# Thirty-two written-out heads, fewer and larger row transfers, two sums buffers, a longer lead and narrower exponentials in a transformer block

## The reference

```
ada = silu(c) @ Wada + bada            # shift, scale, gate for both halves
h   = ln(x) * (1 + scale_msa) + shift_msa
q, k, v = h @ Wq + bq, h @ Wk + bk, h @ Wv + bv      # reshaped to 16 heads of 32
A   = softmax(q @ k.T / sqrt(32))                    # 2048 x 2048 for each of 32 heads
x   = x + gate_msa * ((A @ v) @ Wo + bo)
h2  = ln(x) * (1 + scale_mlp) + shift_mlp
out = x + gate_mlp * (gelu(h2 @ W1 + b1) @ W2 + b2)
```

## Time and profile before

| | us |
|---|---|
| median of 3 runs | 2916.54 |
| lowest and highest of the runs | 2909.09, 2918.22 |
| the profiled execution's own time | 2912.46 |
| its span, first to last instruction | 2910.6 |
| PE busy | 2542.5 |
| POOL busy | 1505.6 |
| DVE busy | 1755.7 |
| ACT busy | 1357.1 |
| mean granted TensorE clock | 0.917 of 2.4 GHz |

### The profile page before, as it was taken

One profiled execution on the slowest core, in us unless ns is written; L12 is line 12 of the kernel. 1 busy time (PEld: TensorE's weight loads), 2 busy tenths in 40 slices (PEclk: granted clock), 3 DMA queues, 4 the chain that ended last, 5 costly groups with the idle time before them and its releaser, 6 DMA issues.

```text
span 2910.6 us, 57655 instructions
## 1 busy us (share of the span) xinstructions
PE 2542.5 (87%) x19544; PEld 1372.6 (47%) x19544; DVE 1755.7 (60%) x2878; ACT 1357.1 (47%) x1598; POOL 1505.6 (52%) x706
## 2 busy tenths in 40 slices
PE   7998868888888888888888888888888887999998
PEld 5787623333333333333333333333333333788887
DVE  5444666666566666666666666666666632665663
ACT  3322145555555555555555555555555544222211
POOL 0000146656667765666676576677566653433220
PEclk9999978989889998899998898999898988999999
DMA  7656442223222222322222232222232111311310
GB/s 260 206 177 172 118 109 50 47 64 70 51 48 47 47 47 67 69 49 47 47 47 48 66 71 47 47 47 47 64 69 50 43 39 49 88 58 58 104 40 29
DMA packets 214223, 211.01 MB, mean 72 GB/s; under 512 B 121600, under 2 KB 154368, under 8 KB 204544
## 3 DMA queue, kind: packets, MB, share of 16 engines
q1 hardware_dynamic: 213232, 207.44, 27.5%
q10 hardware_dynamic: 720, 0.02, 0.0%
HBM read 146.30 MB, written 60.82 MB: 71 GB/s over the span
## 4 chain that ended last, share of the span: by engine, by line
PE 61%; SPq 21%; DMA 6%; issue 5%; DVE 4%; ACT 3%; POOL 0%; ACTq 0%; DVEq 0%; POOLq 0%
PE ps L1245 16%; PE ps L1374 13%; SPq L489 9%; PE ps L1353 7%; SPq L496 6%; PE ps L1490 6%; PE ps L1364 5%; PE ps L1339 4%; PE ps L1355 3%; PE ps L1360 3%; PE ps L1357 2%; SPq L466 2%; SPq L470 2%; DMA partial_sums<-work 2%; DVE part_max L1069 2%
## 5 line engine op out<-in xcount | busy, mean ns | idle before, releaser
L710 POOL TENSOR_TENSOR work<-work 128x1024 f32<-128x1024 f32 x576 | 1353.3, 2386 | 775.4 <-PE ps L1364 464.1
L1069 DVE TENSOR_REDUCE part_max<-ps 128x1 f32<-128x512 f32 x1984 | 1243.4, 683 | 669.0 <-PE ps L1339 666.8
L858 ACT ACTIVATE work<-ps 128x1024 f32<-128x1024 f32 x1024 | 995.6, 1022 | 603.1 <-PE ps L1360 595.9
L1374 PE MATMUL ps<-work 128*32 128x512 f32 x4096 | 610.5, 671 | 0.0
L1339 PE MATMUL ps<-acts_r 32*128 32x512 f32 x1344 | 403.9, 504 | 101.5 <-ACT work L838 84.4
L1245 PE MATMUL ps<-acts_r,weights_r 128*128 128x512 f32 x1536 | 381.2, 398 | 4.9 <-DVE acts_r L989 3.8
L1353 PE MATMUL ps<-acts_r 32*128 32x512 f32 x1408 | 336.0, 504 | 38.6 <-DVE work L1002 18.7
L1353 PEld LDWEIGHTS ps<-acts_r 32*128 32x128 f32 x1408 | 141.6, 199 | 412.8 <-ACT work L858 339.3
L1245 PEld LDWEIGHTS ps<-acts_r,weights_r 128*128 128x128 f32 x1536 | 291.6, 191 | 69.7 <-issue 6.8
L1360 PE MATMUL ps<-acts_r,minus_r 1*128 1x512 f32 x1024 | 237.7, 462 | 65.3 <-DMA acts_r<-max_T 65.3
L1360 PE MATMUL ps<-m_odd,minus_r 1*128 1x512 f32 x1024 | 232.6, 457 | 56.8 <-DMA m_odd<-max_T 56.8
(11 more groups left out here) (88 smaller groups left out, 2478.7 us busy)
## 6 DMA issues: line engine op xcount, KB each, us to landing
acts_r<-k_hi SPq DMA_DIRECT2D x130, 256.0 KB, 4.6
acts_r<-k_lo SPq DMA_DIRECT2D x129, 256.0 KB, 4.8
work<-in_x SPq DMA_DIRECT2D x16, 1024.0 KB, 5.7
q_hi<-work SPq DMA_DIRECT2D x32, 256.0 KB, 2.6
q_lo<-work SPq DMA_DIRECT2D x32, 256.0 KB, 3.3
k_hi<-work SPq DMA_DIRECT2D x32, 256.0 KB, 2.6
k_lo<-work SPq DMA_DIRECT2D x32, 256.0 KB, 3.2
v_rows<-work SPq DMA_DIRECT2D x32, 256.0 KB, 2.0
```

Of the source, the lines that this page charges most:

```text
L710: nc.gpsimd.tensor_tensor(psum_acc[:, at], first, prob[:, t % RING, at], ALU.add).then_inc(add_ok, 1)
L858: nc.scalar.activation(prob[:, t % RING, h * (2 * CH):(h + 1) * (2 * CH)].rearrange("p (j q) -> p j q", q=CH), ps[:, S_BANK + 2 * h:S_BANK ...
L1069: nc.vector.tensor_reduce(part_max[:, r * TT + q // NQ, q % NQ:q % NQ + 1], ps[:, bank, :], AX.X, ALU.max).then_inc(a_max, 1)
L1374: mm = nc.tensor.matmul(ps[j * DH:(j + 1) * DH, O_BANK, :], v_sb[k % TWO][:, t, :], prob[:, t % RING, j * CH:(j + 1) * CH], start=(t == 0) ...
```

## The change

The change has six parts, all in the attention stage.

1. All 32 heads are written out; the loops and their registers are gone.
2. `load_k` is one transfer in place of four: its source is 32 rows read four times over, its destination all 128 partitions. `load_q` is one in place of four as well. The shift rows of a head take four transfers in place of 16.
3. `sums` has two buffers, used in turn, each with its own semaphore (in the last head one buffer alone).
4. The max pass leads by three steps in place of two, so it is complete in step 12; head 0 has three additional quads of it, in steps 2, 6 and 10.
5. ACT's exponentials are 512 wide, four in a step, and PE waits for each score bank by itself.
6. One table lists the uses of all seven banks. PE's order of matmuls within a step is as it was.

```diff
 HI_BUF, TWO = 3, 2
-PERIOD = 6
 M_ROW = 3 * DH
 POOL_TILES = [0, 1, 3, 4, 6, 7, 9, 10, 12, 13]
 PE_TILES = [t for t in range(NT) if t not in POOL_TILES]
 NADD = len(POOL_TILES) - 1
 ND = len(PE_TILES) + 1
 HALVES = 2
-PAIRS = 2
 FILLS = NQ * NT
-LEAD = 2
-EXTRA_AT = (3, 8)
-A_BANKS, S_BANK, O_BANK = 3, 3, 7
+LEAD = 3
+EXTRA_AT = (2, 6, 10)
...
-            tile = (t - 1) % NT
-            if (g or t) and tile in PE_TILES:
-                step["sums"].append((PE_TILES.index(tile), *use("D", 2 if g == G - 1 else None)))
-            if g and t == 1:
-                step["sums"].append((ND - 1, *use("D", 2 if g == G - 1 else None)))
-            steps.append(step)
+            d_bank = 2 if g == G - 1 else None
+            uses = {"extra": [], "max": [None] * NQ, "scores": [use("S", 3 + r) for r in range(NQ)], "sums": []}
+            if g == 0 and t in EXTRA_AT:
+                uses["extra"] = [use("M") for n in range(NQ)]
+            if g < G - 2 or g == G - 2 and t < NT - LEAD:
+                for r in (2, 3, 0, 1):
+                    uses["max"][r] = use("M")
+            tiles = [(t - 1) % NT] if (g or t) and (t - 1) % NT in PE_TILES else []
+            groups = [PE_TILES.index(tile) for tile in tiles] + ([ND - 1] if g and t == 1 else [])
+            uses["sums"] = [(d, *use("D", d_bank)) for d in groups]
+            steps.append(uses)
         heads.append(steps)
-    last_tiles = [(PE_TILES.index(NT - 1), *use("D", 2)), (ND - 1, *use("D", 2))]
-    return heads, last_tiles
...
-        AFTER = ROUNDS * PERIOD + 1
+
+        SUMS_END = USES[G - 1][0]["sums"][0][3]
+
+        def sums_buffer(n):
+            return (n - 1) % 2 if n < SUMS_END else 0
+
+        def sums_before(n, b):
+
+            return sum(sums_buffer(m) == b for m in range(1, n))
...
             def load_k(dst, src, g, done):
-                for r in range(NQ):
-                    sp.dma_start(dst[r * DH:(r + 1) * DH, :].bitcast(F32), src[1][bass.ds(g * DH, DH), :]).then_inc(done, 16)
+                rows = src[1][g * DH:(g + 1) * DH, :].rearrange("(o d) q -> o d q", o=1).broadcast_to((NQ, DH, L))
+                sp.dma_start(dst.bitcast(F32), rows).then_inc(done, 16)
 
             def load_q(dst, src, g, done):
-                for r in range(NQ):
-                    sp.dma_start(dst[r * DH:(r + 1) * DH, :].bitcast(F32), src[0][bass.ds(g * DH, DH), r * CH:(r + 1) * CH]).then_inc(done, 16)
+                rows = src[0][g * DH:(g + 1) * DH, :].rearrange("d (r q) -> r d q", q=CH)
+                sp.dma_start(dst.bitcast(F32), rows).then_inc(done, 16)
 
...
             def put_max(g, u):
 
                 sp.wait_ge(maxT_ok, g + 1)
+                row = m_row[u][0:P:DH, :].bitcast(F32).rearrange("r (s q) -> r s q", q=P)
                 for w in range(MAX_PIECES):
-                    for r in range(NQ):
-                        row = m_row[u][r * DH:r * DH + 1, :].bitcast(F32).rearrange("o (s q) -> o s q", q=P)
-                        sp.dma_start(row[:, :, w * DH:(w + 1) * DH],
-                                     max_T[w * DH + r * TT:w * DH + (r + 1) * TT, :]).then_inc(maxT_in, 16)
+                    sp.dma_start(row[:, :, w * DH:(w + 1) * DH], max_T[w * DH:w * DH + NT, :]).then_inc(maxT_in, 16)
 
...
-            def store_sums(i, g, uses):
+            def store_sums(g, uses):
 
                 for d, _, _, n in uses:
-                    n = i * (PERIOD * ND) + n
+                    b = sums_buffer(n)
                     sp.wait_ge(sums_ok, n)
-                    sp.dma_start(sums_dram[bass.ds(g * ND + d, 1), :].rearrange("o (r q) -> (o r) q", q=CH), sums[0:P:DH, :]).then_inc(sums_out, 16)
+                    sp.dma_start(sums_dram[g * ND + d:g * ND + d + 1, :].rearrange("o (r q) -> (o r) q", q=CH),
+                                 sums[b][0:P:DH, :]).then_inc(sums_out[b], 16)
 
             def load_sums(g):
 
-                sp.wait_ge(sums_out, 16 * ND * (g + 1))
-                sp.dma_start(sums_c[:], sums_dram[bass.ds(g * ND, ND), :].rearrange("n (p x) -> p n x", x=NT)).then_inc(sums_in, 16)
+                done = (USES[g + 1][1]["sums"] if g + 1 < G else USES_END)[-1][3]
+                for b in range(2):
+                    sp.wait_ge(sums_out[b], 16 * sums_before(done + 1, b))
+                sp.dma_start(sums_c[:], sums_dram[g * ND:(g + 1) * ND, :].rearrange("n (p x) -> p n x", x=NT)).then_inc(sums_in, 16)
 
...
+            def take_sums(g, uses):
 
                 for d, bank, _, n in uses:
+                    b = sums_buffer(n)
                     if d < ND - 1:
                         act.wait_ge(pv_mm, START + g * NT + PE_TILES[d] + 1)
                     else:
                         act.wait_ge(den_mm, START + g + 1)
-                    if n > 1:
-                        act.wait_ge(sums_out, 16 * (i * (PERIOD * ND) + n - 1))
-                    nc.scalar.activation(sums, ps[:, bank, :], ACT.Copy).then_inc(sums_ok, 1)
+                    if sums_before(n, b):
+                        act.wait_ge(sums_out[b], 16 * sums_before(n, b))
+                    nc.scalar.activation(sums[b], ps[:, bank, :], ACT.Copy).then_inc(sums_ok, 1)
 
...
 
                     last, gl = ((t - RING) % NT, g if t >= RING else g - 1)
-                    if t >= RING or k:
+                    if gl >= 0:
                         act.wait_ge(pv_mm, START + gl * NT + last + 1)
                         if last in POOL_TILES:
                             act.wait_ge(add_ok, START + gl * (NADD * HALVES) + max(POOL_TILES.index(last), 1) * HALVES)
-                    for h in range(PAIRS):
-                        act.wait_ge(b_mm, g * FILLS + t * NQ + 2 * h + 2)
-                        nc.scalar.activation(prob[:, t % RING, h * (2 * CH):(h + 1) * (2 * CH)].rearrange("p (j q) -> p j q", q=CH),
-                                             ps[:, S_BANK + 2 * h:S_BANK + 2 * h + 2, :], ACT.Exp, scale=SCALE).then_inc(exp_ok, 1)
-                    if k and t == 0:
-                        take_output(i, k - 1)
-                    take_sums(i, g if t > 1 else g - 1, A_USES[k][t]["sums"])
+                    for j, (bank, _, n) in enumerate(USES[g][t]["scores"]):
+                        act.wait_ge(b_mm, n)
+                        nc.scalar.activation(prob[:, t % RING, j * CH:(j + 1) * CH], ps[:, bank, :], ACT.Exp, scale=SCALE).then_inc(exp_ok, 1)
+                    if g and t == 0:
+                        take_output(g - 1)
...
+            def bank_free(use):
+
+                bank, before, _ = use
                 if before:
                     kind, n = before
-                    if kind == "M":
-                        pe.wait_ge(a_max, i * (PERIOD * FILLS) + n)
+                    if kind == "S":
+                        pe.wait_ge(exp_ok, START + n)
+                    elif kind == "M":
+                        pe.wait_ge(a_max, n)
                     else:
-                        pe.wait_ge(sums_ok, i * (PERIOD * ND) + n)
-
```

More of the change, by code:

```diff
@@ L62, with bank_table @@
 COL = P // 4
-LOADS_HI, LOADS_LO, LOADS_0 = 8, 9, 6
+LOADS_HI, LOADS_LO, LOADS_0 = 2, 3, 6
 MAX_PIECES = 4
-def a_sequence():
-    count = {"M": FILLS, "D": 0}
-    last = [None] * A_BANKS
+def bank_table():
+    last = [None] * BANKS
+    count = {"S": 0, "M": FILLS, "D": 0}
     turn = 0
-    heads = []
     def use(kind, bank=None):
@@ L77, in use @@
         if bank is None:
-            bank = turn % A_BANKS
+            bank = turn % 3
             turn += 1
+        before = last[bank]
         count[kind] += 1
-        before = last[bank]
         last[bank] = (kind, count[kind])
         return bank, before, count[kind]
+    heads = []
     for g in range(G):
@@ L87, in a_sequence @@
         for t in range(NT):
[L88 to L91, removed]
-            tile = (t - 1) % NT
-            if (g or t) and tile in PE_TILES:
-                step["sums"].append((PE_TILES.index(tile), *use("D", 2 if g == G - 1 else None)))
-            if g and t == 1:
-                step["sums"].append((ND - 1, *use("D", 2 if g == G - 1 else None)))
-            steps.append(step)
+            d_bank = 2 if g == G - 1 else None
[9 more added lines that the diff above has]
+            steps.append(uses)
         heads.append(steps)
-    last_tiles = [(PE_TILES.index(NT - 1), *use("D", 2)), (ND - 1, *use("D", 2))]
-    return heads, last_tiles
-A_USES, A_LAST = a_sequence()
+    end = [(d, *use("D", 2)) for d in (PE_TILES.index(NT - 1), ND - 1)]
+    return heads, end
+USES, USES_END = bank_table()
 assert NT - 1 in PE_TILES
@@ L165, in block_kernel @@
         bv_rows = view(work, 3072, D)
-        sums = view(work, 3072, CH)
+        sums = [view(work, at, CH) for at in (3072, 1024)]
         o_st = [view(work, at, CH) for at in (2048, 2560)]
@@ L271, in block_kernel @@
         sums_ok = sem("sums_ok")
-        sums_out = sem("sums_out")
+        sums_out = [sem(f"sums_out{b}") for b in range(2)]
         sums_in = sem("sums_in")
@@ L577, in _ @@
```

(26 more changed lines are left out.)

235 lines of the change are left out of this document (108 added, 127 removed).

## The result

The changed kernel takes 3029.61 us (median of 3 runs, 3022.74 to 3038.69) against 2916.54: the ratio is 1.040 (95% interval 1.034 to 1.045), so slower by 3.4 to 4.5%. The forecast was 2930 with a range of 2850 to 3190. The time lies in the range, and the waits came where they were worked out, at steps 3 and 6, but together they were longer: the increase was 113 us, not 13. The direction was little more than an even guess, as slower had a chance of 0.49.

What follows compares the result with a forecast made beforehand. Two stalls per head, 7.3 and 6.3 us, from waits for SP's transfers were to give way to one at step 6. 2912.5 + 3 (30 heads) + 11 (outside them) = 2926.5, or 2930 on the median's scale; range 2850 to 3190.

Steps and rivals of the forecast that it cites:

- Shift rows: SP's hand-over at the head boundary: four transfers take 2.5 us, 7.4 less than the 16 before.
- stall A: Head boundary of the kernel before: ACT idles while PE waits for shift rows; 7.3 us per head, forecast to go.
- Four engines: One-transfer k and q loads run on four of 16 DMA engines, 12.9 us against 5.1; chance 0.66.
- The rival of sixteen engines: Loads follow the destination and keep 5.1 us; both stalls go, 51.9 us a head, 2565 us; chance 0.14.
- The high part's load: First load in a head: 0.314 us a packet, 12.9 us with q; step 0's store lands at about 15.0.
- the packets stay slow: Rival for the k loads: 0.55 us a row, a head grows by 15 us, near 3400 us; chance 0.10.
- SP is not held: Rival: output stores are accepted at once, step 1's store lands 2.5 us earlier per head, 2855 us; chance 0.10.
- Exponentials: ACT: four of 512 take 2.10 us, 0.15 more; plain step 3.05 us, nine cost 1.4 us a head.
- The slow steps behind a stall: The step after the step 6 wait was again taken at 4.98 us, as in the kernel before.
- Written-out heads: Heads without loops and registers: taken at nothing, bounds of -1 and +1 us a head.
- The start: Before head 0: +10.5 us from the q store behind head 0's k loads, -2.8 around the v stores.
- Head 0: Its late weights queue behind two loads, 15 us more, mostly hidden; taken at +6 us (0 to 15).

Runs made afterwards that it cites:

- four_loads: The changed kernel with the k and q loads by four transfers each again, all else as changed: 2545.69 us, ratio 0.873.
- four_exp1024: four_loads with two exponentials of 1024 in a step in place of four of 512: 2526.77 us, ratio 0.867.
- four_lead2: four_loads with the max pass two steps ahead in place of three: 2539.34 us, ratio 0.871.
- four_shift16: four_loads with 16 transfers for the shift rows, lead of three kept: 2652.29 us, ratio 0.910.
- two-engine run: The changed kernel with each k and q load as two transfers, source outer dimension two: 3770.8 us, one run.

## Why the prediction was right in kind and short in size

*Shift rows and stall A: right.* The hand-over takes 2.31 us (2.5 worked out), the idle time at the boundary is 0.57, and L492 is not in the chain.

*Four engines: right.* The windows show 25% of 16. The Trainium skill, DMA: Bandwidth & Descriptors, section "Why a DMA increments its semaphore by 16 and not by 1", gives as the number of engines the largest up to 16 that divides the slowest dimension of both sides. The trace agrees: 25% with a four and 12.6% with a two against 128 and 64 partitions fit that rule, and the times of the three splits, 2545.69, 3029.61 and 3770.8 us, go the same way. The rival of sixteen engines had priced what four_loads then showed: 51.9 us a head and 2565, measured 51.0 and 2545.69.

*The high part's load: the term that was mis-sized.* The step said "On each of four engines 32 x 0.314 + 32 x 0.089 = 12.9 us" and let step 0's store land 15.0 us into the head. It landed at 1436.99 - 1416.30 = 20.7, because a packet of the high part took 0.465 us. So step 3 waited 8.5 us in place of 2.6. By that duration the load would take 32 x 0.465 + 32 x 0.089 = 17.7 us, 4.8 more than worked out, of the 5.7 by which the store was late (an estimate from one window). The low parts, behind another load, kept to 0.311. Step 1's store landed at 1452.20 - 1416.30 = 35.9 (32.2 worked out), step 6 waited 4.9 in place of seven, and this head took 66.7 us where 63.3 stood. The text had this as the rival "the packets stay slow", half of which it called as well possible: over all heads the excess is 66.0 - 63.3 = 2.7 us, 82 in all. The forecast's own part of the range ended at 0.40 us a packet; the high part alone is above it, and the mean of the two parts, 0.388, is just inside, because the low part was quick. That was not foreseen.

*The rival "SP is not held": it fell.* SP was held longer than before, 10.7 + 18.1 us a head against 6.4, with fewer transfers outstanding. It seems to be the pieces queued on the four engines, not the number of transfers, that it stands behind.

*Exponentials: nearly right.* Four take 2.06 to 2.07 us (2.10 worked out); a plain step is 1470.19 - 1467.24 = 2.95 us (3.05). Nine of them against 2.90 would be 0.45 us a head, 14 in all; four_exp1024 says 19.

*The slow steps behind a stall: right in price, without the reason.* The working carried 4.98 us over from the kernel before and had no term for the clock that makes them. It came out at 4.82 and 4.94, because the new stalls also brought the granted clock down to 0.50.

*Written-out heads* were taken at nothing and were not tried alone. Four_loads' head was 0.9 us under the sum of its parts, so they don't seem to cost; nothing more is shown.

*The start: the second term that was short,* +23.9 us where +10.5 and -2.8 stood. (The second is a slip: its own terms, 7.4 and 2.8 gained and 12.9 - 5.1 lost, give -2.4.) The chain of the changed kernel in order of time, to be set beside the earlier trace rows:

```profile
313.55 24.57 DMA q_lo<-work
...
373.85 22.07 DMA v_rows<-work
```

The first starts 1.8 us later and is 24.57 - 9.36 = 15.2 us longer, where +10.5 was worked out from packets of 0.314 us; slower packets would do that, but the other transfers in this stretch don't let them be read alone. From its end to the start of the second there are 45.0 us before and 35.7 now, 9.3 gained where 7.4 + 2.8 = 10.2 were forecast. The second is 22.07 - 5.88 = 16.2 longer, and here the working was short: I had let the high parts of head 1 cost the difference of two loads, 7.8 us, but SP was held for 23.2 us while it handed over the three v stores behind them. Together 1.8 + 15.2 - 9.3 + 16.2 = 23.9. Head 0 lost 9.7 (+6, with 15 as its bound); ACT waits 11.22 us for one of the late weights, until 432.69, and waited for none of them in head 0 before.

*What the change was worth without its loads.* Against 2915 us: 2545.69, or 370 us less. With all else in place the second buffer is worth 183 and the four shift transfers 107; the narrow exponentials cost 19, and the longer lead cannot be told from nothing (6 us the wrong way). Their sum, 183 + 107 - 19 - 6 = 265, is not the 370, but it counts stall A too low. The four transfers remove stall A with a lead of two as well (four_lead2), and with 16 transfers the lead of three had already taken part of it (four_shift16). If the transfers get all of stall A, 7.3 us in 31 heads or 226 us, the sum is 183 + 226 - 19 - 6 = 384, near the 370. That is an estimate; 16 transfers with a lead of two and four-part loads were not run, and neither was the written-out code by itself.

## What to carry to other kernels

Count the engines that a transfer will use before merging transfers: one transfer whose outer dimension is four runs on a quarter of the engines, and if the small stores have an outer dimension of four too, they stand behind it. Fewer hand-overs were worth having where SP's time was on the path and the transfers were small (the shift rows, 107 us), and not where they cost engines (the loads, 484 us lost). When large loads can't be avoided, hand over the small transfers first, all of them: with the load of the sums left behind the high parts the kernel was 139 us slower than the changed one, and with that load and the stores up to step 3 ahead of them 174 us faster. And look at the granted clock behind a stall of PE: in the changed kernel each stall cost about 2 us more than its length.

## What the runs showed of the hardware that I had not expected

- An 8 KB packet has no one duration: 0.465, 0.495 and 0.468 us in loads that started on idle engines, 0.311 in one right behind another, on the same four engines, 0.397 and then 0.317 within one load, and 0.310 on two engines (0.126 x 64 / 26 from 1470 to 1474 us of the two-engine run). The cause stays open; four engines that read the same row in step at first and drift apart later would fit, and it was not tried.
- A queue of few large transfers holds SP as well as one of many small ones: a single v load took 10.73 us to hand over where 0.43 is enough in four_loads.
- Two q loads a head of 256 KB each, on four engines, cost 36 us over 32 heads, though k's loads, four times as large, were spread out.
- A wait of PE is paid twice: in this kernel the granted clock was 0.50 to 0.54 in the step behind each, and 32 matmuls took 4.66 to 4.78 us in place of 2.94.
